# Two norms folded into the next products, a transform in halves, and the first routing weights spread by PE

## What is computed

```
x = x + attn(layernorm(x))        # 16 heads of 8, softmax, qkv product with bias, output product
x = x + xattn(layernorm(x), ctx)  # correlation by rfft / irfft over 64 positions, top 4, softmax, roll of V
x = x + moe(layernorm(x))         # 8 experts, hidden 256, sigmoid gate with bias, top 2, relu squared
layernorm(v) = (v - mean(v)) / sqrt(var(v) + 1e-5)
```

## Time and profile before

| | |
|---|---|
| median of 3 runs | 143.54 us (143.08 to 144.1) |
| profiled execution | 142.93 us |
| its span | 141.2 us |
| PE busy | 123.0 us (87%) |
| VectorE busy | 104.1 us (74%) |
| ScalarE busy | 54.9 us (39%) |
| POOL busy | 38.5 us (27%) |
| mean granted TensorE clock | 0.976 of 2.4 GHz |

### The profile page before, as it was taken

One profiled execution on the slowest core, in us unless ns is written; L12 is line 12 of the kernel. 1 busy time (PEld: TensorE's weight loads), 2 busy tenths in 40 slices (PEclk: granted clock), 3 DMA queues, 4 the chain that ended last, 5 costly groups with the idle time before them and its releaser, 6 DMA issues.

```text
span 141.2 us, 4101 instructions
## 1 busy us (share of the span) xinstructions
PE 123.0 (87%) x1612; PEld 104.9 (74%) x1612; DVE 104.1 (74%) x341; ACT 54.9 (39%) x117; POOL 38.5 (27%) x71
## 2 busy tenths in 40 slices
PE   6749987856899998697899839999999999999992
PEld 2246556545788886585798836999989899999991
DVE  1349999999999879999797969836938664073711
ACT  2203354635517703172513034754325344170550
POOL 8579190460302020406663030411500300000000
PEclk9978999999999999999999986999999999999999
DMA  4888800000000000000000610610017172001001
GB/s 121 263 225 295 358 14 0 7 0 5 5 5 0 0 7 7 0 2 5 0 5 1 250 49 5 260 42 0 0 39 241 63 237 102 0 0 37 5 2 37
DMA packets 5027, 9.50 MB, mean 67 GB/s; under 512 B 368, under 2 KB 3856, under 8 KB 4240
## 3 DMA queue, kind: packets, MB, share of 16 engines
q1 hardware_dynamic: 4432, 8.50, 17.5%
q10 hardware_dynamic: 576, 0.73, 1.8%
HBM read 8.68 MB, written 0.56 MB: 65 GB/s over the span
## 4 chain that ended last, share of the span: by engine, by line
PE 51%; DVE 25%; issue 5%; DMA 4%; ACT 1%; POOL 1%; DVEq 0%
PE ps L845 21%; PE ps L834 14%; DVE negm L497 5%; DVE feat L492 4%; PE ps L785 4%; DVE low L503 3%; DMA wb_sb<-w_dram 3%; PE ps L821 2%; DVE nat L481 2%; DVE wtop L602 2%; PE ps L800 1%; DVE onat L511 1%; PE ps L792 1%; DVE topi L555 1%; PE ps L731 1%
## 5 line engine op out<-in xcount | busy, mean ns | idle before, releaser
L641 DVE SCALAR_TENSOR_TENSOR rel<-ps,wb_sb 128x512 f32<-128x512 f32 x32 | 21.8, 690 | 13.1 <-PE ps L834 7.2
L845 PE MATMUL ps<-wdn_sb,hid 128*128 128x128 f32 x256 | 30.6, 276 | 0.0
L430 ACT ACTIVATE hid<-rel 128x512 f32<-128x512 f32 x32 | 20.2, 631 | 25.1 <-DVE rel L641 16.9
L845 PEld LDWEIGHTS ps<-wdn_sb,hid 128*128 128x128 f32 x256 | 29.5, 192 | 0.3 <-issue 0.2
L834 PE MATMUL ps<-xhi,whi 128*128 128x256 f32 x64 | 19.2, 300 | 0.1
L834 PE MATMUL ps<-xhi,wlo 128*128 128x256 f32 x64 | 17.8, 278 | 0.0
L834 PE MATMUL ps<-xlo,whi 128*128 128x256 f32 x64 | 17.8, 278 | 0.0
L372 ACT ACTIVATE prob<-ps 128x512 f32<-128x512 f32 x16 | 9.1, 599 | 9.4 <-PE ps L731 9.4
L343 POOL TENSOR_TENSOR mix<-w,con 128x128 f32<-128x128 f32 x16 | 6.1, 412 | 23.3 <-DVE w L585 23.3
L834 PEld LDWEIGHTS ps<-xhi,whi 128*128 128x128 f32 x64 | 12.1, 189 | 0.5 <-issue 0.4
L834 PEld LDWEIGHTS ps<-xlo,whi 128*128 128x128 f32 x64 | 12.1, 189 | 0.0
(11 more groups left out here) (103 smaller groups left out, 211.3 us busy)
## 6 DMA issues: line engine op xcount, KB each, us to landing
wb_sb<-w_dram SPq DMA_DIRECT2D x4, 1024.0 KB, 4.7
wup_sb<-w_up SPq DMA_DIRECT2D x1, 1024.0 KB, 6.0
wdn_sb<-w_down SPq DMA_DIRECT2D x1, 1024.0 KB, 8.0
c_sb<-ctxt SPq DMA_DIRECT2D x2, 256.0 KB, 6.8
out<-x_sb SPq DMA_DIRECT2D x4, 128.0 KB, 1.8
con<-consts SPq DMA_DIRECT2D x1, 400.0 KB, 3.0
wmid_sb<-w_mid ACTq DMA_DIRECT2D x1, 324.0 KB, 5.8
row_sb<-rows ACTq DMA_DIRECT2D x1, 260.0 KB, 4.9
```

The lines of the kernel that those rows point to most:

```text
L430: nc.scalar.activation(hid[:, a % 3, :], rel[:, a % 2, :], ACT.Square).then_inc(done["sq"], 1)
L641: nc.vector.scalar_tensor_tensor(rel[:, a % 2, :].rearrange("p (c t) -> p c t", c=2), psum("up", a).rearrange("p (c t) -> p c t", c=2), 0. ...
L845: last = mm(acc_ps[:, D * t:D * (t + 1)], hid[:, a % 3, 2 * P * half + P * t:2 * P * half + P * (t + 1)], wdn_sb[:, e, half, :], start=(e ...
```

## The change

Four things change, and with them the order on all engines and the banks.

1. **First norm.** `nm1` is gone. PE transposes raw x. The mean is taken out of the weights: `mean_of` is a matrix of 1/128, PE multiplies the qkv weights by it (`cent.0.0`) and VectorE subtracts the result from them; `cent.0.1` does the same for the query weights. rstd is multiplied in by `qkv` on VectorE, which becomes a two-operation step.
2. **Second norm.** `nm2` is gone. ScalarE scales the rows of the forward transform by rstd (`fw`, two instructions a chunk), and `dft` multiplies raw `x12` by that. `dft` now waits for `wo` and `fw`.
3. **Inverse transform.** `corr` becomes two halves, each 64 rows deep and 128 columns wide, in two banks: six products in place of three. The parts that were left out are zeros.
4. **Routing weights of chunk 0.** `wt.0` writes the 8 rows four times, at partitions 0, 32, 64 and 96, ScalarE copies each. `spread` is eight products, 8 rows deep, 128 wide and 256 columns long, which give every partition the weights; ScalarE copies the four banks (`spread.0.0` to `spread.0.3`) into `wb_sb`. Chunks 1 to 3 go through DRAM as before.

```diff
@@ ScalarE
+                if name == "fw":
+                    act.wait_ge(done["rs2"], a + 1)
+                    if a == 0:
+                        act.wait_ge(ld_con, 16)
+                    if a >= 2:
+                        act.wait_ge(full["dft"], a - 1)
+                    for t in range(2):
+                        last = nc.scalar.activation(fw[:, a % 2, t], con[:, C_FWD:C_FWD + 2 * 2 * NF], ACT.Identity,
+                                                    scale=rstd[:, CHUNKS + a, t:t + 1])
+                    last.then_inc(fw_ready, 1)
...
                 if name == "wt":
                     act.wait_ge(full["wt"], a + 1)
-                    nc.scalar.copy(wT[:, a], psum(name, a)[0:EXPERTS, 0:2 * P]).then_inc(done[name], 1)
+                    for r in range(QUAD if a == 0 else 1):
+                        last = nc.scalar.copy(wT[32 * r:32 * r + EXPERTS, a], psum(name, a)[32 * r:32 * r + EXPERTS, 0:2 * P])
+                    last.then_inc(done[name], 1)
+                if name == "spread":
+                    act.wait_ge(full["spread"], 1)
+                    nc.scalar.copy(wb_sb[:, 0, 2 * part:2 * part + 2].rearrange("p e n -> p (e n)"), psum(name, 0, part)).then_inc(done[name], 1)
@@ VectorE
+                if name == "cent":
+                    dve.wait_ge(full["cent"], part + 1)
+                    w = wmid_sb[:, W_Q:W_Q + D] if part else wqkv_sb[:]
+                    nc.vector.tensor_tensor(w, w, psum(name, 0, part)[:, 0:(D if part else 3 * D)], ALU.subtract).then_inc(done[name], 1)
                 if name == "qkv":
                     t = part
+                    dve.wait_ge(done["rs1"], a + 1)
...
-                    nc.vector.tensor_tensor(nat[:, t, :, :, 32 - HD:32].rearrange("p c j d -> p (c j) d"), proj, bias,
-                                            ALU.add).then_inc(done["qkv"], 1)
+                    nc.vector.scalar_tensor_tensor(nat[:, t, :, :, 32 - HD:32].rearrange("p c j d -> p (c j) d"), proj,
+                                                   rstd[:, a, t:t + 1], bias, ALU.mult, ALU.add).then_inc(done["qkv"], 1)
...
@@ PE
                 if name == "dft":
-                    pe.wait_ge(done["nm2"], a + 1)
+                    pe.wait_ge(done["wo"], a + 1)
+                    pe.wait_ge(fw_ready, a + 1)
...
-                        last = mm(spec[:, :, t, :], xn[:, 2 * a + t, :],
-                                  con[:, C_FWD:C_FWD + 2 * 2 * NF].rearrange("p (i f) -> p i f", i=2), start=True, stop=True)
+                        last = mm(spec[:, :, t, :], x12[:, 2 * a + t, :], fw[:, a % 2, t].rearrange("p (i f) -> p i f", i=2),
+                                  start=True, stop=True)
...
-                    c_ps = bank(name, a)
+                    halves = [bank(name, a, two) for two in range(2)]
                     for i in range(3):
-                        last = mm(c_ps[:, 0:NB * L], prod[:, a % 2, i, :], con[:, C_INV + NB * L * i:C_INV + NB * L * (i + 1)],
-                                  start=(i == 0), stop=(i == 2))
+                        for two in range(2):
+                            rows = slice(2 * NF * two, 2 * NF * (two + 1))
+                            at = C_INV + NB * L * i + 2 * L * two
+                            last = mm(halves[two][:, 0:2 * L], prod[rows, a % 2, i, :], con[rows, at:at + 2 * L], start=(i == 0),
+                                      stop=(i == 2))
...
+                if name == "spread":
+                    pe.wait_ge(done["wt"], 1)
+                    quads = [bank(name, 0, r) for r in range(QUAD)]
+                    for half in range(2):
+                        for r in range(QUAD):
+                            e = 2 * r + half
+                            row = con[32 * r:32 * r + EXPERTS, C_ID + 32 * r + e:C_ID + 32 * r + e + 1].broadcast_to([EXPERTS, P])
+                            last = mm(quads[r][:, 2 * P * half:2 * P * (half + 1)], row, wT[32 * r:32 * r + EXPERTS, 0, :], start=True,
+                                      stop=True)
...
@@ order on PE, first words of the list
-        warm.12.0 xt.0.0 cdft.0.0 qkv.0.0 qkv.0.1 xt.1.0 xt.2.0 cproj.0.0 qkv.1.0 qkv.1.1 vtr.0.0 qkv.2.0 vtr.0.1 qkv.2.1
+        warm.12.0 xt.0.0 cent.0.0 xt.1.0 cent.0.1 qkv.0.0 qkv.0.1 qkv.1.0 qkv.1.1 xt.2.0 xt.3.0 cdft.0.0 qkv.2.0 qkv.2.1 vtr.0.0
```

More of the change, by code:

```diff
@@ L45 @@
 C_LEN = C_IOTA + 8
-MATMULS = ("xt", "cdft", "cproj", "qkv", "score", "pt", "vtr", "pv", "vt2", "wo", "dft", "qp", "corr", "g", "ov", "y2",
+MATMULS = ("cent", "spread", "xt", "cdft", "cproj", "qkv", "score", "pt", "vtr", "pv", "vt2", "wo", "dft", "qp", "corr", "g", "ov", "y2",
            "xt3", "gate", "wt", "up", "down")
-EVACS = ("xt", "cdft", "cproj", "qkv", "pt", "vtr", "pv", "vt2", "wo", "dft", "qp", "corr", "g", "ov", "y2", "xt3", "gate",
-         "wt", "up", "sq", "fin", "rs1", "rs2", "rs3", "nm1", "nm2", "nm3")
+EVACS = ("cent", "spread", "xt", "cdft", "cproj", "qkv", "pt", "vtr", "pv", "vt2", "wo", "dft", "qp", "corr", "g", "ov", "y2", "xt3", "gate",
+         "wt", "up", "sq", "fin", "rs1", "rs2", "rs3", "nm3")
@@ L59 @@
[L59 to L62, removed]
@@ new lines @@
+        pt.3.1 dft.2.0 pt.3.2 qp.2.0 pt.3.3 pv.3.0 pv.3.1 corr.2.0 xt3.0.0 gate.0.0 g.1.0 vt2.3.0 ov.1.0 wo.3.0 up.0.0 y2.1.0
+        wt.0.0 up.1.0 g.2.0 up.2.0 spread.0.0 ov.2.0 dft.3.0 xt3.1.0 up.3.0 y2.2.0 gate.1.0 down.0.0 qp.3.0 down.1.0 down.2.0
+        down.3.0 corr.3.0 xt3.2.0 up.4.0 wt.1.0 gate.2.0 up.5.0 up.6.0 up.7.0 down.4.0 down.5.0 down.6.0 down.7.0 wt.2.0 up.8.0
+        up.9.0 g.3.0 up.10.0 up.11.0 up.12.0 ov.3.0 up.13.0 down.8.0 y2.3.0 down.9.0 down.10.0 down.11.0 down.12.0 down.13.0
@@ L95 @@
+        rs2.3.0 rs3.1.0 xsp.1.0 rs3.2.0 xsp.2.0 mix.3.0 rs3.3.0 xsp.3.0""",
     "SP": """
[L96 removed]
+        wdma.1.0 store.0.0 wdma.2.0 store.1.0 wdma.3.0 store.2.0 store.3.0""",
 }
 BANK_TEXT = """
[L99 to L100 removed]
@@ L137, in opened @@
         return [(name, a, r) for r in range(QUAD)] if part == 0 else []
+    if name == "corr":
+        return [(name, a, 0), (name, a, 1)]
+    if name == "spread":
+        return [(name, a, r) for r in range(QUAD)]
     if name == "pv":
@@ L543, in _ @@
                 if name == "top":
-                    corr = psum("corr", a)[:, 0:NB * L].rearrange("p (b s) -> p b s", s=L)
+                    corr = [psum("corr", a, b // 2)[:, L * (b % 2):L * (b % 2 + 1)] for b in range(NB)]
                     if part == 0:
@@ L664, in released @@
                     pe.wait_ge(done["vtr"], 2 * a + part + 1)
+                elif name in ("cent", "spread"):
+                    pe.wait_ge(done[name], part + 1)
                 elif name == "acc":
@@ L820, in _ @@
                     for t in range(2):
-                        last = mm(t_ps[0:EXPERTS, P * t:P * (t + 1)], wtok[:, a, t, :], ident, start=True, stop=True)
+                        for r in range(QUAD if a == 0 else 1):
+                            last = mm(t_ps[32 * r:32 * r + EXPERTS, P * t:P * (t + 1)], wtok[:, a, t, :], ident, start=True, stop=True)
+                    last.then_inc(full[name], 1)
+                if name == "spread":
+                    pe.wait_ge(done["wt"], 1)
[6 more added lines that the diff above has]
+                                      stop=True)
                     last.then_inc(full[name], 1)
```

157 lines of the change are left out of this document (85 added, 72 removed).

## The result

The changed kernel takes **135.69 us** (median of 4 runs, 134.97 to 136.47); the kernel before, on the same chip, 143.74. The ratio is **0.9447 [0.9373, 0.952]** (in brackets the 95% interval): 8.0 us less, where 6.0 were forecast; the time lies inside the range of 134.6 to 141.5. The profiled execution has 135.17 us and a span of 133.4, against 142.93 and 141.2, so the two traces differ by 7.8 us and account for nearly the whole. The runs of the kernel after fall in two groups by the mean granted clock: 135.17 and 134.97 us at 1.00, 136.22 and 136.47 at 0.987. Experiments 7 and 8 are about that.

What follows compares the result with a forecast made beforehand. VectorE bounds 17.62 to 75.34 us, PE 87.58 to 138.46, with a stop between. Start, VectorE's stretch, the way to the downs and PE's rest put PE's end at 132.4: 143.54 - 6.0 = 137.5 us, range 134.6 to 141.5.

Steps and rivals of the forecast that it cites:

- The start: Before VectorE's full stretch: wtop.0.0 moves from 17.62 to 16.37, when w_up lands, -1.25 us.
- VectorE's stretch, its work: From wtop.0.0 to the end of pick.0: 4.8 us of steps go out, 2.9 come in, net -1.9 us.
- VectorE's idle time: In the same stretch: 2.4 us idle before, 1.5 us taken as left, -0.9 us.
- The path behind `wo`: st2, rs2, fw, dft, copy, qp: estimated 3.6 us; nothing waits if queues add no more than 2.4 us.
- From `wtok` to the end of `down.3`: Chunk 0's wtok at 71.3, rel.0 at 75.4, down.0 at 78.2, down.3 ending at about 82.2.
- The rest on PE: What follows down.3 takes 50.2 us, so PE ends at 132.4 instead of 138.46.
- inner range: Span of the unknown terms: 135.2 us (no idle, all overlaps) to 139.8 (2 us more idle).
- Small matmuls without overlap: On PE, spread, wt.0 and corr.3 do not overlap: +2.5, +1.2, +0.67, 141.9 us; chance 0.14.
- A wait in place of the second norm: VectorE waits on the fold's path: 140.5 us at 0.75 a chunk, 146.3 at 2.2; chances 0.12 short, 0.06 long.
- A stop at chunk 1: The stop moves to chunk 1, whose weights still go by DRAM, if the load exceeds 8 us: 141.8 us; chance 0.05.
- That it does not do what it says: Some other wait holds the downs until the old time: 143 to 143.5 us; chance 0.03.
- no granted clock under 1.0 after 17 us: A sign of the forecast on TensorE: its clock stays full after 17 us.

Runs made afterwards that it cites:

- Experiments 7 and 8: Kernel after with matmuls of zeros in TensorE's gap at 52 us, 135.64 us; with the first wtop pair behind ft.1.1, 135.38 us; with both, 134.87 us.
- experiment 5: Kernel after with the second norm as VectorE's nm2 steps again, without fw on ScalarE: 138.56 us, 0.961.
- experiment 6: Kernel before with both wtop pairs behind the ft steps, 144.09 us; kernel after with its second wtop pair moved beside GpSimd's vpar, 136.41 us.
- experiment 3: Kernel after with the inverse transform whole again, three products of 128 rows and 256 columns: 137.47 us, 0.9546.
- experiment 1: Kernel after with chunk 0's routing weights through DRAM again, without spread and the fourfold wt.0: 140.99 us, 0.9651.
- experiment 2: Kernel after with chunk 0's routing weights through DRAM and ten matmuls of zeros on PE in the stop: 137.35 us, 0.9496.

## Why the prediction was right

The path was right at every step that it named. Four sizes were off. The largest two, in VectorE's stretch, brought 2.5 us more than forecast; two smaller ones behind it took 1.0 back. Without that offset the time would have been near the low end of the range.

- **The start**: -1.25 forecast, -1.49 measured. The wait is for `w_up`, as said; the DMA took 5.69 us instead of 6.0. The centring costs nothing: PE and VectorE do it in VectorE's wait for x. That it came so near is in part luck. In the other traces of the new order that keep this place, `wtop.0.0` starts anywhere from 15.76 to 17.16 us, and the wait is 0 to 1.28 us, by when the load lands.
- **VectorE's stretch, its work**: -1.9 forecast, 55.34 - 52.00 = -3.34 measured, and this was the term most mis-sized. The removed and added steps were priced well, `nm2` for one: 0.50 to 0.52 us a step (experiment 5) against 0.50. What the prediction missed is that the steps that stayed did not keep their durations. The two `wtop` pairs went from 2.68 to 1.64 us (start to start 2.5 to 1.5) because the second no longer lies beside `vpar` and the first only for 0.29 us (experiment 6). One `vals` pair took 0.92 us beside `vpar` before, and none takes over 0.49 now. Against it, `biased` and `wtok` lost about 0.65 us in the same way, and `qkv` with rstd takes 593 ns instead of 535.
- **VectorE's idle time**: -0.9 forecast, -1.93 measured. It had been put between -2.4 and +2.0, with 1.5 us left over, a choice and no sum; 0.45 are left, in gaps too small to have a releaser (the wait for `w_up`, 0.45 us by chance as well, lies ahead of the stretch). Gone are the two waits of the trace before, 0.94 us for `wo` and 0.66 ahead of a norm step. The path behind `wo` with `fw` in it did not make VectorE wait at all. Whole transforms would have cost a wait of 0.6 us here (experiment 3), so the halves have a share in it that the prediction had put at nothing.
- **From `wtok` to the end of `down.3`**: 10.9 forecast, 80.06 - 68.58 = 11.48 measured. `wt.0` took 0.62 (0.6), `spread` 1.12 (1.0); `up.1`, the first `up` after `wt.0`, took 0.91 on the chain instead of 0.68. (From its start to that of `g.2` it takes 0.82, and 0.81 in experiment 1, where `wt.0` is not fourfold, so that is not the cause.) `rel.0` came 4.6 us behind `wtok` (4.1), `down.0` 2.8 behind `rel.0` (2.8).
- **The rest on PE**: 50.2 forecast, 50.63 measured, 0.20 of it `corr.3` (0.87 instead of 0.67: alternating row groups overlap, but not fully).

The sum: -1.49 - 5.27 = -6.76 at `wtok`, where -4.05 was forecast; behind it 11.48 + 50.63 us where 63.12 were before, so -1.0, where -2.0 was forecast; -7.8 in all.

The ends of the prediction's inner range, 135.2 and 139.8, do not follow from its own terms. It had taken 1.5 us of idle time and counted the overlaps of `corr` and `spread` in full, so no idle time gives 137.5 - 1.5 = 136.0, and 2 us more than before give 137.5 + 2.9 = 140.4. The measured 135.69 lies just under the first: no choice of the idle time reaches it, and the shorter `wtop` is the term that was lacking.

**The rivals.** Small matmuls without overlap: no, though `corr` comes out between the two values. A wait in place of the second norm: no, there is none. A stop at chunk 1: no, the load lands in time in this trace. That it does not do what it says: no. Of the prediction's signs one came in part: no granted clock under 1.0 after 17 us holds in this trace, but other executions had the spell near 56 us. Experiment 1 puts the spread at some 3 us, and by experiment 2 probably more than half of it is TensorE's clock. The prediction had the same order of things, but since it followed one stretch into the next it never had to say how much each part brought. Taken alone, the parts were: the spread 2.0% of the time of before, the second norm 1.6%, the halves 1.0% (differences of ratios of different sets, each uncertain by 0.9 to 1.0%, so the last is barely clear of nothing). The first norm was not tried alone. The start, with its better clock, is 1.49 us by the traces.

One thing came that the prediction did not count. TensorE ran at 1.2 GHz from 9 to 12 us before and at 2.4 GHz after. In the trace before it had stood idle for 2.41 us, until the context had landed for `cdft.0`:

```profile
8.95 1.19 PE L702 MATMUL ps<-con,c_sb 128*128 128x128 f32 x4 [2.41 <-DMA c_sb<-ctxt]
```

In the new order the centring, two transposes of raw x and the first `qkv` stand ahead of `cdft.0`, and PE was busy for the whole microsecond from 8 to 9. The windows, before and then after:

```profile
8.00:9.00 1.00, 0.05 (x1) 0.08 (x1) 0.59 (x4) 0.00 (x0) 0.91 (x2) 0.79 1.00 250
9.00:12.00 3.00, 3.00 (x9) 2.37 (x10) 2.33 (x11) 0.59 (x1) 2.90 (x5) 0.50 0.70 185
```

```profile
8.00:9.00 1.00, 1.00 (x7) 0.73 (x6) 0.80 (x5) 0.37 (x1) 0.81 (x2) 1.00 1.13 279
```

How much it gave was not tried; in the new order the landing of `w_up` ended the start anyway.

## What to carry to other kernels

When an order changes, look at what each long VectorE step has beside it on GpSimd, before and after: a pair that nobody touched gained 0.6 us here, and a short step lost 0.4. A DMA round trip on the path of TensorE cost more than its length, since the engine ran at half its clock behind it; filling the stop with idle matmuls got back some 2 of 3 us, and taking the round trip away got all. And small matmuls on two halves of the array's rows took 72 ns apiece where neighbours in the stream used different halves, and 99 where they did not: order them so that they alternate.
